# First attention of a two-layer network: queries and keys fetched during the projection, W2's transform in two places, peaks and scores in other PSUM banks and another order

## What is computed

```python
Q = (x @ W_q).reshape(b, s, 16, 32)             # 16 query heads
K, V = (x @ W_k), (x @ W_v)                     # 4 heads each, used by 4 query heads
scores = rope(Q) @ rope(K).T / 32 ** 0.5        # per head, no mask: 1024 x 1024
out = softmax(scores) @ V @ W_o
...
hidden = fwht(silu(x @ W1.T) * (x @ W3.T))      # Walsh-Hadamard transform over 2048
out = hidden @ W2.T
```

## Time and profile before

| | us |
|---|---|
| median of three runs | 2746.16 |
| the profiled execution, its own time | 2746.78 |
| its span, first to last instruction | 2745.0 |
| PE busy | 2525.7 (92%) |
| DVE, ACT, POOL busy | 1754.8, 1081.3, 1023.4 |

### The profile page before, as it was taken

One profiled execution on the slowest core, in us unless ns is written; L12 is line 12 of the kernel. 1 busy time (PEld: TensorE's weight loads), 2 busy tenths in 40 slices (PEclk: granted clock), 3 DMA queues, 4 the chain that ended last, 5 costly groups with the idle time before them and its releaser, 6 DMA issues. The chain is left out here.

```text
span 2745.0 us, 35908 instructions
## 1 busy us (share of the span) xinstructions
PE 2525.7 (92%) x12212; PEld 1711.3 (62%) x12212; DVE 1754.8 (64%) x4115; ACT 1081.3 (39%) x2569; POOL 1023.4 (37%) x756
## 2 busy tenths in 40 slices
PE   7889899898769999999697999969999979999998
PEld 3334344343258888888575777756777656667886
DVE  6467667585335555555646999947999823335886
ACT  2225445353422333222214777725767721111111
POOL 2418757575711111110004676624444410001442
PEclk9979999999989999999899999999999999999999
DMA  7651302120020000000212101010000078882101
GB/s 226 209 130 24 66 12 55 24 55 1 16 92 16 15 30 15 15 0 1 93 43 74 51 21 32 21 39 23 14 5 15 1 270 294 296 296 88 57 24 62
DMA packets 167335, 193.64 MB, mean 71 GB/s; under 512 B 51982, under 2 KB 114446, under 8 KB 166784
## 3 DMA queue, kind: packets, MB, share of 16 engines
q1 hardware_dynamic: 155648, 178.90, 20.9%
q0 software_dynamic: 11520, 12.64, 1.5%
HBM read 161.95 MB, written 54.53 MB: 79 GB/s over the span
## 5 line engine op out<-in xcount | busy, mean ns | idle before, releaser
L692 DVE TENSOR_REDUCE mx<-bank 128x1 f32<-128x512 f32 x512 | 326.3, 678 | 123.9 <-PE bank L599 119.3
L539 POOL TENSOR_TENSOR probs<-probs 128x1024 f32<-128x1024 f32 x128 | 301.7, 2378 | 211.8 <-PE bank L622 165.7
L750 ACT ACTIVATE probs<-bank 128x1024 f32<-128x1024 f32 x256 | 250.1, 1023 | 274.0 <-PE bank L612 274.0
L1546 POOL TENSOR_SCALAR mix<-mix,sm 128x256 f32<-128x256 f32 (+1 forms) x256 | 232.6, 920 | 175.2 <-DVE sm L1443 174.8
L1486 ACT ACTIVATE ms<-ms,sm 128x256 f32<-128x256 f32 (+1 forms) x512 | 247.6, 486 | 94.1 <-DVE sm L1414 93.2
L599 PE MATMUL bank<-k_parts,q_parts 96*128 96x512 f32 x512 | 216.4, 474 | 10.1 <-DVE mx L692 4.7
L599 PEld LDWEIGHTS bank<-k_parts,q_parts 96*128 96x128 f32 x512 | 93.5, 195 | 170.8 <-DVE mx L692 138.9
L926 POOL TENSOR_TENSOR up_lo<-up_raw,up_hi 128x1024 fp32r<-128x1024 f32 x16 | 46.1, 2902 | 402.3 <-ACT up_hi L916 402.3
L1414 DVE CUSTOM_DVE_ANT_0 ms<-bank,misc 128x256 f32<-128x256 f32 (+1 forms) x512 | 184.7, 399 | 2.4
L612 PE MATMUL bank<-q_parts,k_parts 97*128 97x512 f32 x512 | 148.2, 405 | 15.4 <-ACT probs L750 8.9
L996 DVE TENSOR_TENSOR hid<-bank,sg 128x512 f32<-128x512 f32 x64 | 44.2, 691 | 180.4 <-ACT sg L946 180.4
(11 more groups left out here) (227 smaller groups left out, 5873.0 us busy)
## 6 DMA issues: line engine op xcount, KB each, us to landing
ewg<-in_L_ffn_Wg_dram SPq DMA_DIRECT2D x32, 704.0 KB, 6.8
ewu<-in_L_ffn_Wu_dram SPq DMA_DIRECT2D x32, 704.0 KB, 8.0
ewd<-in_L_ffn_Wd_dram SPq DMA_DIRECT2D x32, 512.0 KB, 5.2
q_parts<-qk_dram SPq DMA_DIRECT2D x48, 256.0 KB, 4.5
up_raw<-in_L_ffn_W_dram SPq DMA_DIRECT2D x16, 512.0 KB, 4.4
ewd<-in_L_ffn_Wd_dram SPq DMA_DIRECT2D x32, 192.0 KB, 5.4
qk_dram<-qk_hi SPq DMA_DIRECT2D x4, 1280.0 KB, 5.5
qk_dram<-qk_lo SPq DMA_DIRECT2D x4, 1280.0 KB, 8.0
```

Of the source, the lines that this page charges most:

```text
L539: pool.tensor_tensor(probs[:, even, half, :], probs[:, even, half, :], probs[:, odd, half, :], ALU.add).then_inc(S["paired"], 1)
L692: dve.reduce_max(mx[:, U % 2, q, h:h + 1], bank[:, h, :], AX.X).then_inc(S["max"], 1)
L750: act.activation(probs[:, s % BUFS, 2 * x:2 * x + 2, :], bank[:, 2 + 2 * x:4 + 2 * x, :], ACT.Exp, scale=scale).then_inc(S["exps"], 1)
L1546: pool.tensor_scalar(mix[:, p % 2, h, 0:w], mix[:, p % 2, h, 0:w], sm[:, p % 3, 8 + h:9 + h], None, ALU.mult).then_inc(S["probs"], 1)
```

## The change

- `project0` keeps `hi` and `lo` as a ring of four row blocks. SP stores each row block by its own two DMAs. During block c = 1 SP also loads the first queries (four loads of three DMAs), and at the start of c = 2 the keys of the first batch. W2 and `wo` are no longer loaded here, and SP no longer waits at the end: `heads0` waits for the stores of the last column block, then loads the other keys, the first part of W2, and `wo`. POOL sets the keys' row of ones at the start of `project0`.
- Peaks: both halves of a query block follow each other into one of two pairs of banks (0 and 1, or 2 and 3), and DVE reduces both with one operation straight to `neg`. `mx` and its last reduction are gone; SP waits on `max`.
- Scores: one bank each, 4 and 5 in turn, and one exp for each.
- PE's order in a step becomes score, peaks, score, values, two scores, sums on odd steps, peaks. A projection comes one a step, in steps 2 to 5, behind the second score and in bank 0; both peaks then come last.
- W2: the sums and differences come first, on parts fetched from the input, 16 of them in 13 of 14 slots (`PERIOD`), and the two buffers swap roles from part to part. The Hadamard products come last, two at the end of each of steps 118 to 125 (`flatten`), copied out by DVE, with W2 coming and going in pieces of two tiles (512 KB) through a ring of four in the same space.
- Two semaphore updates that nobody waited on (`cos`, `padded`) are left out.

The core of the diff:

```diff
@@ project0, SP @@
             for c in range(NC):
-                wait(sp, S["hi"], (c + 1) * NR)
-                sp.dma_start(env["qk"][0, :, :, c * CH:(c + 1) * CH], hi[:, c % 2, :, :].bitcast(F32)).then_inc(S[f"staged{c % 2}"], 16)
...
-            for half in range(2):
-                wait(sp, S[f"staged{half}"], 16 * NC)
-            wait(sp, S["wo"], 16)
-            wait(sp, env["fw"]["given"], 16 * (D // CW))
+                for f in range(NR):
+                    store(c, f)
+                    if c == 1 and f < QT0:
+                        stored(0, f)
+                        queries(env, sp, t, 0, f)
+                    if c == 2 and f == 0:
+                        stored(0, QT0)
+                        stored(1, QT0)
+                        keys(env, sp, t, 0)
@@ project0, ACT @@
                 for f in range(NR):
+                    n = c * NR + f
+                    wait(act, S["rotated"], n + 1)
+                    if n >= KEPT:
+                        wait(act, S[f"staged{n % KEPT}"], 32 * (n // KEPT))
+                    act.activation(hi[:, n % KEPT, :], rot[:, f % 2, :], ACT.Copy).then_inc(S["hi"], 1)
@@ heads0, SP @@
+                for f in range(QT0 + 1):
+                    staged(NC - 1, f)
+                keys(env, sp, t, 1)
                 fetch(0)
+                sp.dma_start(wo[:, :, :], env["ins"]["L0_attn_W_o"].rearrange("(k p) n -> p k n", p=P)).then_inc(
+                    env["p0"]["wo"], 16)
                 for U in range(HEADS):
-                    wait(sp, S["neg"], U + 1)
+                    wait(sp, S["max"], (U + 1) * SUBS)
...
-                    if U % 16 == 5 and U > 16:
-                        store(U // 16 - 1)
-                        fetch(U // 16)
+                    if U >= PERIOD and U % PERIOD == HPT:
+                        store(U // PERIOD - 1)
+                        if U // PERIOD < PARTS0:
+                            fetch(U // PERIOD)
+                    if U == HEADS - 3:
+                        wait(sp, F["stored"], 16 * PARTS0)
+                        for n in range(RING):
+                            pair_in(n)
+                for n in range(HT0 // 2):
+                    wait(sp, F["flat"], 2 * n + 2)
+                    sp.dma_start(env["w2"][:, 2 * n:2 * n + 2, :], ring[:, n % RING, :, :]).then_inc(F[f"slot{n % RING}"], 16)
+                    m = n - 1
+                    if m >= 0 and m + RING < HT0 // 2:
+                        wait(sp, F[f"slot{m % RING}"], 32 * (m // RING + 1))
+                        pair_in(m + RING)
@@ heads0, PE @@
+                    wait(pe, S["max"], n - 1)
+                    for h in range(2):
+                        mm = pe.matmul(bank[:, 2 * (n % 2) + h, :], qp[0:R, u, q * P:(q + 1) * P],
+                                       kp[b][0:R, u % KV0, h * CH:(h + 1) * CH], start=True, stop=True)
+                    mm.then_inc(S["peaks"], 1)
+                def score(V, s, j):
+                    b, U = V // (TURNS // BATCH), HPT * V + j
+                    wait(pe, S["exps"], HPT * (V * QB + s) + j - 1)
+                    if s == 0:
+                        wait(pe, S[f"shift{j}"], 64 * (V + 1))
+                    pe.matmul(bank[:, 4 + j % 2, :], kp[b][0:R + 1, U % KV0, s * P:(s + 1) * P],
+                              qp[0:R + 1, U % UN0, :], start=True, stop=True).then_inc(S["scored"], 1)
...
+                        N = V * QB + s
+                        n = 2 * N + LEAD * SUBS
+                        projects = cc and V % QT0 == 1 and 2 <= s < 2 + SUBS
                         score(V, s, 0)
+                        if not projects:
+                            peaks(n)
                         score(V, s, 1)
+                        if projects:
+                            wait(pe, S["max"], min(n, SLOTS0) - 1)
+                            project(cc - 1, s - 2, 0)
+                        if N:
+                            values((N - 1) // QB, (N - 1) % QB)
+                        score(V, s, 2)
+                        score(V, s, 3)
+                        if s % 2 and N > 1:
+                            sums(N // 2 - 1)
+                        if projects:
+                            wait(pe, S["added"], (cc - 1) * SUBS + s - 1)
+                            peaks(n)
+                        peaks(n + 1)
+                        if 0 <= N - FLAT < HT0 // 2:
+                            flatten(2 * (N - FLAT))
+                            flatten(2 * (N - FLAT) + 1)
@@ heads0, DVE @@
+                    if q == 0:
+                        wait(dve, S[f"shift{U % HPT}"], 64 * (U // HPT))
+                    wait(dve, S["peaks"], n + 1)
+                    dve.tensor_reduce(neg[:, U % HPT, q:q + 1], bank[:, 2 * (n % 2):2 * (n % 2) + 2, :], AX.XY, ALU.max,
+                                      negate=True).then_inc(S["max"], 1)
```

More of the change, by code:

```diff
@@ L492, in _ @@
[L492 to L498, removed]
                 def fetch(j):
-                    wait(sp, F["stored"], 16 * j)
-                    sp.dma_start(home[:, :, :], part(j)).then_inc(F["got"], 16)
+                    wait(sp, F["mixed"], 16 * j)
+                    sp.dma_start(bufs[j % 2], env["ins"]["L0_ffn_W2"].rearrange("(h p) d -> p h d", p=P)[
+                        :, :, j * CW:(j + 1) * CW]).then_inc(F["got"], 16)
@@ L577, in _ @@
                         slot = (V * QB + s) // 2
-                        for k in MIXES.get(slot % 16, ()):
-                            mix(slot // 16 * 16 + k)
+                        j, m = slot // PERIOD, slot % PERIOD
+                        if j < PARTS0 and m:
+                            for n in range(16 * (m - 1) // (PERIOD - 1), 16 * m // (PERIOD - 1)):
+                                mix(16 * j + n)
                         if V and s == QB - 1:
@@ L660, in _ @@
                     for s in range(QB):
-                        U, q = HPT * V + LEAD + s // 2, s % 2 * 2
-                        last = (V, s - 1) if s else (V - 1, QB - 1)
-                        after_y = None
-                        if cc and V % QT0 == 1 and s % 4 == 0:
-                            for half in range(2):
-                                project(cc - 1, s // 2 + half, min(2 * U * SUBS, 2 * HEADS * SUBS))
-                            after_y = (cc - 1) * SUBS + s // 2
-                        peak(U, q, 0, after_y)
@@ L684, in _, with maximum @@
[L684 removed]
+                    project(NC - 1, q, q)
             @block.vector
             def _(dve):
[L688 to L689 removed]
+                def maximum(n):
+                    if n >= SLOTS0:
                         return
[L691 to L692 removed]
@@ L710, in invert, with add, flattened @@
                         inv.then_inc(S["rec"], 1)
-                def add(cc, q):
+                def add(cc, q, to):
                     wait(dve, S["y"], cc * SUBS + q + 1)
                     row = X[:, cc * SUBS + q, :]
-                    dve.tensor_tensor(row, row, bank[:, q % 2, :], ALU.add).then_inc(S["added"], 1)
-                for U in range(LEAD):
-                    for q in range(SUBS):
-                        maximum(U, q, 0)
-                        maximum(U, q, 1)
-                    negate(U)
+                    dve.tensor_tensor(row, row, bank[:, to, :], ALU.add).then_inc(S["added"], 1)
+                def flattened(n):
+                    wait(dve, F["raw"], n + 1)
+                    dve.tensor_copy(ring[:, n // 2 % RING, n % 2, :], bank[:, n % 4, :]).then_inc(F["flat"], 1)
+                for n in range(LEAD * SUBS):
+                    maximum(n)
                 for V in range(TURNS):
@@ L762, in take_sums @@
                     act.activation(den[:, :], bank[:, 7, :], ACT.Copy).then_inc(S["d_taken"], 1)
-                for n in range(4 * (D // CW)):
-                    wait(act, F["raw"], n + 1)
-                    act.activation(t["w2"][:, n // 4, 4 * (n % 4):4 * (n % 4) + 4, :],
-                                   bank[:, 2 + n % 4, :].rearrange("p (a n) -> p a n", n=CW),
-                                   ACT.Copy).then_inc(F["flat"], 1)
-                wait(act, F["kept"], 16 * (D // CW))
                 for V in range(TURNS):
```

230 lines of the change are left out of this document (99 added, 131 removed).

## The result

The changed kernel takes **2697.82 us**, the median of four runs (2696.93 to 2698.5), beside 2745.36 for the kernel before on the same chip: a ratio of 0.9827 with a 95% interval of 0.9810 to 0.9844, some 47.5 us faster. The forecast was 2675, range 2650 to 2710: sign and range hold, and a third of the expected gain is missing. The profiled spans, 2745.0 and 2696.7, differ by 48.3.

| | before | after | difference | forecast |
|---|---|---|---|---|
| first score | 177.02 | 152.36 | -24.7 | -35.5 |
| first score to first score of the last step | 553.94 | 536.94 | -17.0 | -32.6 (terms 2 to 4) |
| from there to the next layer's first work | 33.21 | 30.06 | -3.2 | -3.3 |
| the rest of the program | | | -3.5 | 0 |

A forecast was written before the change was run, and what follows sets the result against it. PE, busy 92% of the span, was taken as the bound, losing time to DVE and POOL. Terms -35.5 - 17 - 25 + 9.4 - 3.3 = -71.4 took 2746.2 to 2675 us, range 2650 to 2710.

The forecast's parts named there:

- Term 1: Start of the first attention: earlier PE entry, no Hadamard products there, faster peak slots; -35.5 us (-25 to -39).
- the slot of 1.3: Lead before the first score: each two-peak slot takes 1.3 us instead of 1.57, with DVE reducing two banks at once.
- the shifts: Before the first score: tiny shift DMAs, queued behind other loads, cost 0 to 4.5 us; taken as 0.
- Term 2: Ten plain turns of eight steps in the steady stretch: 29.0 us each against 30.6; -17 us (-31 to +9).
- turns stay: Rival, plain turns: waits for DVE become waits for exps, a turn is again 30.6 us; 2697 us, chance 0.17.
- DVE: no wait: Plain turns: two reductions of 1.13 to 1.29 us per step, sometimes an inversion, never make a peak slot wait.
- Term 3: Three projection turn pairs: the 6.46 us wait for POOL's norm and half clock go; -25 us (-10 to -35).
- Term 4: Last steps: eight steps take two Hadamard products each, W2's pieces arriving hidden; +9.4 us (+7 to +20).
- Term 5: Tail: no mix behind the last pair, which starts earlier, so norm ends sooner; -3.3 us (-1 to -4).
- POOL late: Rival, turns: first mixes wait for W2 or double slots make sums late, some 25 us more; 2700 us, chance 0.12.
- Clock: Rival, turns: one 10 us dip to half clock per turn, +80 us; 2755 us, chance 0.03.
- Two banks as one: Rival, scores: each waits for the exp just before it, a turn is 36.5 us; 2772 us, chance 0.03.

The follow-up runs named there:

- e1: The changed kernel with POOL's two memsets moved from the start to behind its fourth and eighth subtraction: 2691.05 us, ratio 0.9797.
- e4: The changed kernel with both the moved memsets of e1 and the product order of e3: 2666.6 us, ratio 0.9704.
- e3: The changed kernel in the order score, score, values, sums on odd steps, score, score, then both slots of peaks: 2673.15 us, ratio 0.9732.
- e8: e4 with DVE's inversion put behind both maxima of a step instead of between them: 2660.62 us, ratio 0.9695.
- e10: e8 with the third score of odd steps issued between values and sums: 2678.0 us.
- e2: The changed kernel with the sums of odd steps directly behind the values, ahead of the third and fourth score: 2690.45 us, ratio 0.9795.
- e5: The changed kernel with the projections of a turn in its steps 0 to 3 instead of 2 to 5: 2717.8 us, ratio 0.9904.
- e7: The kernel before, with each of DVE's maxima over the first 256 of 512 columns of a bank: 2721.27 us, ratio 0.9916.

## Why the prediction was right or wrong

**Term 1** (-35.5; was -24.7). The step that failed is "POOL's memset moves to before its first subtraction, where it is idle: nothing". It asked whether POOL was free, not who else was at work then: DVE was, in an instruction that the memset shuts out. That took 6.2 of the 10.8, as delay: 20.90 for 14.71. It is also what the time says: e1 is 6.8 faster than the changed kernel, e4 6.6 faster than e3.

Another 3.0 can't be laid on the memset. From the first of the 24 products to the end of the group of eight behind them it takes 21.5 in the changed kernel's execution and 20.9 in e8, which has no early memset, but 18.5 to 19.1 in nine of the other ten kernels, with the memset and without (in e10 17.0). In the changed kernel's group of 24 the weight loads are 0.85 apart up to 26.2 and 0.43 after it, as between half and full clock, though the table gives 1.00 granted there; why is open. So e2, e3 and e5, with the same code up to there, begin the peaks at 124.48 to 125.01 and not at 127.48. Another 1.0 is that PE starts 1.3 after the projection's last copy, not 0.3. The rest stood: the slot of 1.3 (1.21 for the reduction; 24.9 for the lead, 0.6 over the forecast), the shifts (0.31), the stores, and the covered load.

**Term 2** (29.0 a turn; was 30.4, within its bounds and almost at the rival "turns stay"). In time it is the largest miss: the ten turns gained 1.4 us instead of 17. The mechanism was counted rightly, three returns in two steps and one exp wait; the mis-sized term is the return, 0.2 instead of 0.30 to 0.32. The way in was missed: in the earlier trace rows the second peaks' 0.82 - 0.47 was put down to DVE as a whole, but 0.10 of it is the change of kind in the last product before values. Three times 0.12 is 0.36, and the exp wait was 0.24 instead of 0.2; less the 0.25 of oT's copy, for which the rows leave no room (4 x 7.61 is the whole turn), this makes 4 x 0.40 - 0.25 = 1.35 of the 1.4. The turn so kept its length for another reason than before: it got rid of DVE's wait (e7 put it at 1.9 a turn) and spent the gain on a third round trip and the exp wait. The two changes of order in e3 and e8 take 1.3 and 0.75 of that back. "DVE: no wait" held for this order, not for e3's. One reading was wrong without harm: not ten but seven of the old turns take 30.6; the sum's ten are these seven and one turn of each pair.

**Term 3** (17.2 extra a turn; 16.2, from 46.65 - 30.4; before it was 24.2, the mean of three pairs). Right in its reason: e5 brought the wait and the half clock back. That it came to -24.3 of -25 is in part luck, as two errors cancel: the extra fell by 8.0 a turn and not by 6.6, and the plain gain inside the term was 0.4 instead of 5.1.

**Term 4** (+9.4; +11.9 for the last two turns together). W2's 32 listed products lie between 653.18 and 686.72 with no wait of PE for a piece; sized a little low, with the plain steps again in it. **Term 5** (-3.3; -3.2). Right. That turn 0 gains nothing was wrong: it gained 3.3.

**The rivals.** "Turns stay", 2697, has nearly the measured turn, but only half by its own reason: the exp waits are there, at a quarter of a microsecond per two steps. That it has the measured time is luck: the start's 10.8, which no rival had, are nearly made up by turn 0, the projection turns and the rest of the program. "POOL late" didn't come: its mixes fit, and PE waited for it only at the very end, before the last sums (2.24) and for the last norm (5.66). "Clock" didn't come either: 1.00 from 159.7 to 699.1. What the Trainium skill, TensorE: Matmul & The Clock Gate, section "A second HAM failure mode: psum-queue depth-cycling", reports of another kernel, a clock that falls and rises with small gaps between groups, isn't seen here. "Two banks as one" would have shown each score waiting; one wait of 0.24 in two steps is far from it.

Open are what lengthens the first products by some 3 us in one execution and not in another, and the 3 to 4 us ahead of layer 1's attention.

## What to carry to other kernels

An engine that is idle isn't thereby free: before an instruction is moved, look at what the engines beside it do in that very stretch, and for POOL at DVE above all. On PE count how often the order changes between full-width products and those of 32 columns, and keep the small ones of a step together and complete. When a wait goes, add up the new order's own parts again from start to start; the gain may go to what the reordering costs.

## What the runs showed of the hardware that I hadn't expected

- A memset of one partition, 4096 elements, took POOL 3.6 us and held DVE's scaling of 128x512 for all of it (3.7 instead of 0.55).
- A round trip between products of 128 and of 32 columns cost 0.30 us at full clock, of which a third falls on the product before the change.
- Four products of 32 columns side by side and two of them alone both kept PE for about 1.0 us.
